# Hybrid Mamba/MoE layer on one core: squares kept in PSUM, other PSUM banks and weight slots around the gate stage, and six products moved from GpSimd to VectorE

## The chip, the cores and the metric

One NeuronCore of a Trainium2 chip. The metric is the device time of one launch in microseconds (us). The names of the engines: PE is TensorE, ACT is ScalarE, DVE is VectorE, POOL is GpSimd, SP issues DMAs.

## The reference, cut to what matters

The layer is `x + mixer(norm(x))`, then a mixture of experts, a block-sparse projection and the same mixture again. The change touches the mixer alone. Per group of heads (8 groups of 16 heads of 64 channels) it computes, cut:

```python
zxbcdt = hidden_states @ in_proj_w.T                    # gate, x, B, C, dt
xBC = silu(causal_conv4(xBC) + conv_b)
Gm = einsum('bcihn,bcjhn->bhcij', C, B)
Y_diag = einsum('bhcij,bcjhd->bcihd', Gm * L, xs)       # L = exp(segment_sum(A dt))
Y_off = einsum('bckhn,bchdn,bhck->bckhd', C, states, state_decay)
y = (Y_diag + Y_off + D * x) * silu(gate)
var = mean(y * y over the group's 1024 channels)
y = y * rsqrt(var + EPS) * norm_w
return y @ out_proj_w.T
```

There are 1024 tokens (2 sequences of 512). `Gm * L` is the decay-score product, `y * y` the squares.

## The kernel before, in words

The whole kernel is one program per engine, written out by hand with counted semaphores; nothing schedules it. The mixer is a loop over the 8 groups (`Fori(0, GROUPS)` in each engine's block). Inside, the order of the work is a fixed sequence of steps, k = 0 to 47 (called ticks here); every engine walks through the same k in its own program and takes from each tick what is its own, so an engine may be several ticks behind another. Semaphores named with `now` wait for a count of this group, `before` for one of the group before; an engine executes strictly in its order, so what stands behind a waiting instruction waits too.

- **Big units** on PE (loop over k, L1515 on): one unit is 12 matmuls of 128x512 into one PSUM bank (3 passes of a hi/lo split times 4 parts of the contraction), or 24 in the output stage. k = 0 to 19 are the convolution inputs (`NCONV`; B, C and eight x tiles, two sequences each), k = 20 to 35 the 16 gate tiles (n = k - 20), k = 36 to 43 the output projection (t = k - 36, halves m = 0 and 1). `big_bank(k)` is k % 3, and unit k waits for whoever reads unit k - 3.
- **Small units** on PE behind each big one, for head units u = 0 to 15: state matmuls at k = u + 10 (bank `ST` = 6), transposes at k = u + 8 (banks 3 and 5), the diagonal matmuls L1603 at k = u + 11 (bank `DG` = 4), which need both decay-score products of u, and the off-diagonal ones L1617 (bank `OF` = 7).
- **ACT**: first tap and tanh of the convolution (L880, L888), the decay tiles (L900, L852), the hi parts of weights (L862), tanh of the gate (L912), the squares (L925) at tick n + 22, and the hi parts `ah` of the output stage (L933).
- **DVE**: taps and the end of the convolution (L1184, L1193: unit k is finished in DVE's tick k + 1), `xs` (L1152), states (L1167, L1172), diagonal and off-diagonal results (L1209, L1215), the gate's (tanh + 1) * gate (L1221) at tick n + 20, the sum of the squares (L1230) at tick n + 23, `al` (L1233), and the lo parts of the output weights (L1139), one per tick.
- **POOL**: y += off-diagonal (L652), `xd` (L664), both decay-score products of a unit (L678, at tick u + 10, counted by `lg_ok`), lo parts of weights (L685), y *= gate (L702, at tick n + 21).

A square goes to `acc` for the first two gate tiles, else to `sq`, half of the SBUF tile `quad`, two slots; DVE adds it to `acc` two steps later:

```python
dst = sq[:, n % 2, :] if tile else acc[:, b, :]
```

Weights pass through 11 slots (`W_SLOT`) at ticks given by `W_TICK`; the last of the eight output pieces has tick 36.

Of the kernel before, what the change touches and what calls it, by code (L numbers as in the profile page):

```python
# [33 lines left out]
def hybrid_layer(nc, x_d, wconv_d, wgate_d, wout_d, wdt_d, cpar_d, gpar_d, dtb_d, alog_d,  # L34
# [8 lines left out]
    with ctx:  # L43
# [30 lines left out]
        sq = quad[:, 0, :].rearrange("p (n s) -> p n s", n=2)  # L74
# [67 lines left out]
        TR, DG, ST, OF = (3, 5), 4, 6, 7  # L142

# [74 lines left out]
        lg_ok = counted("lg_ok", 2 * UNITS)  # L218
# [85 lines left out]
        def phase_end(eng, n):  # L304
# [6 lines left out]
        W_SLOT = [0, 1, 2, 3, 4, 5, 6, 7, 8, 9, 2, 3, 4, 5, 0, 1, 8, 9, 2, 3, 4, 5, 6, 7, 10, 8]  # L311
# [4 lines left out]
            + [28, 29, 30, 31, 32, 33, 34, 36]  # L316
# [26 lines left out]

        def big_bank(k):
            return k % 3

        def big_bank_free(eng, i, k):

            q, wait = (k - 3, now) if k >= 3 else (max(q for q in range(NBIG) if q % 3 == k), before)
            if q < NCONV:  # L350
                wait(eng, conv_ok, i, q + 1)
            elif q < NCONV + NGATE:
                wait(eng, gate_ok, i, q - NCONV + 1)
            else:
                wait(eng, res_ok, i, q - NCONV - NGATE + 1)
# [241 lines left out]
        def _(pool):  # L597
# [45 lines left out]
            with pool.Fori(0, GROUPS) as i:  # L643
                for k in range(NBIG + 4):
# [114 lines left out]
        def _(act):  # L759
# [69 lines left out]
            with act.Fori(0, GROUPS) as i:  # L829
                for k in range(NBIG + 4):  # L830

                    if k - T_G in (1, 2):
                        b = k - T_G - 1
                        tr_done(act, i, f"G{b}")
                        if b == 0:
                            before(act, lg_ok, i, 2 * UNITS)
                        inc(nc.scalar.activation(G[:, b * CH:(b + 1) * CH, :], b4(tr_bank(f"G{b}")), ACT.Copy,
                                                 scale=0.25), g_act)
# [15 lines left out]
                    for p in range(PIECES):  # L854
                        if W_TICK[p] == k:
                            raw_arrived(act, i, p)
                            w_slot_free(act, i, p)
                            kt = p - (PIECES - XT)
                            if kt == 0:
                                act.wait_ge(gpar_in, 16 * (i + 1))  # L860
                            scale = gpar[:, kt:kt + 1] if kt >= 0 else 1.0
                            inc(nc.scalar.activation(wh[:, W_SLOT[p], :], raw[:, R_SLOT[p], :], ACT.Copy,  # L862
                                                     scale=scale), w_hi)

                    if k < NCONV:
# [156 lines left out]
        def _(dve):  # L1022
            credit(dve, (wo_lo, ss_add, taps, conv_ok, xs_ok, s_step, s_ok, off_ok, ydiag_ok, gate_ok, dcol_ok,
# [108 lines left out]
            with dve.Fori(0, GROUPS) as i:  # L1132
                for k in range(NBIG + 4):

                    for p in range(PIECES - XT, PIECES):
                        if W_TICK[p] == k:
                            kt = p - (PIECES - XT)
                            now(dve, w_hi, i, p + 1)
                            inc(STT(wl[:, W_SLOT[p], :], raw[:, R_SLOT[p], :], gpar[:, kt:kt + 1],  # L1139
                                    wh[:, W_SLOT[p], :], ALU.mult, ALU.subtract), wo_lo)  # L1140

# [75 lines left out]

                    if NCONV <= k < NCONV + NGATE:
# [5 lines left out]
                    n = k - 3 - NCONV  # L1224
                    if BATCH <= n < NGATE:
                        b = GATES[n][1]
                        now(dve, sq_ok, i, n + 1)
                        if n > BATCH:
                            now(dve, ss_add, i, n - BATCH)
                        inc(TTn(acc[:, b, :], acc[:, b, :], sq[:, n % 2, :], ALU.add), ss_add)  # L1230
# [230 lines left out]
        def _(pe):  # L1461
# [49 lines left out]
            with pe.Fori(0, GROUPS) as i:  # L1511
                for k in range(NBIG):
# [38 lines left out]
                    if 0 <= u < UNITS:  # L1551
# [4 lines left out]
                        else:  # L1556
                            before(pe, s_ok, i, UNITS)
# [300 lines left out]
```

How the kernel before makes its waits and increments, by code:

```python
        def row_arrived(eng, i, n):  # L246
            q = n % LR
            eng.wait_ge(row_in[q], (i * len(range(q, 2 * UNITS, LR)) + n // LR + 1) * 16)
# [1 line left out]
        def e_arrived(eng, i, u):  # L250
            q = u % ER
            eng.wait_ge(e_in[q], (i * len(range(q, UNITS, ER)) + u // ER + 1) * 32)
# [39 lines left out]
        def now(eng, name, i, n):  # L292
            eng.wait_ge(per[name][0], per[name][1] * (i + 1) + n)
# [1 line left out]
        def before(eng, name, i, n):  # L296
            eng.wait_ge(per[name][0], per[name][1] * i + n)
# [5 lines left out]
        def phase_end(eng, n):  # L304
            eng.drain().then_inc(phase, 1)
            eng.wait_ge(phase, 4 * n)
# [26 lines left out]
        def raw_arrived(eng, i, p):  # L334
            n = R_SLOT[p]
            eng.wait_ge(raw_in[n], (i * R_COUNT[n] + R_SLOT[:p + 1].count(n)) * 16)
# [105 lines left out]
        @block.sync  # L442
        def _(sp):
            xv = x_d.rearrange("(t p) h -> p t h", p=P)
            for n in range(4):
                sp.dma_start(X[:, 2 * n:2 * n + 2, :], xv[:, 2 * n:2 * n + 2, :]).then_inc(x_in[n], 16)
            sp.dma_start(raw[:, 3, :], wdt_d).then_inc(dtw_in, 16)
            sp.dma_start(dtb[:, :], dtb_d).then_inc(par_in, 16)
            sp.dma_start(alog[:, :], alog_d).then_inc(par_in, 16)
            sp.dma_start(rraw[:, :, :], wr_d).then_inc(rt_in, 16)
            sp.wait_ge(dve_self, 1)
            with sp.Fori(0, GROUPS) as i:
                before(sp, taps, i, 3 * NCONV)
# [515 lines left out]
            def t_rows_evac(run, tau):  # L970
                act.wait_ge(tx_mm, job(run, tau) + 1)
                if tau >= 2:
```

## Time and profile before

| | us |
|---|---|
| median of 3 runs (2179.29 to 2180.45) | 2179.96 |
| the profiled execution | 2181.42 |
| its span, first to last instruction | 2179.7 |
| PE busy / DVE / ACT / POOL | 2003.3 / 1502.7 / 1178.5 / 1086.9 |
| one group of the mixer | 207 to 209, eight of them |

The mixer's eight groups take about 1.67 ms of the 2.18. PE is busy 92% of the span, and its granted clock is 0.976 of full speed on average. Starts are in microseconds from the first instruction. Matmuls overlap, so each is shown longer (0.39) than the distance to the next (0.227). "Idle before, releaser" names the instruction whose end let the waiting one go.

### The profile page before, as it was taken

Reading aid. Unit: us, or ns where it says so; the run is one execution under the profiler, and the core shown is the slowest. Engines: PE = TensorE matmul, PEld = TensorE weight load, DVE = VectorE, ACT = ScalarE, POOL = GpSimd, SP = SyncE. Lnnn points to the kernel's source line nnn. Section 1 sums busy time; section 2 is a strip of 40 time slices with the busy share of each in tenths; the row PEclk is TensorE's granted clock in tenths of the full one; section 3 lists DMA queues with packets and bytes.
Section 4 is the critical chain, followed back from the end, with each engine's and each line's share of the span. In section 5 each row is a group of like instructions: output and inputs, shape, how many; then the busy total and the mean of one; then the engine's idle time right before and its main releaser. Section 6 shows DMA issues by size and latency. Waiting matters only on the chain.

```text
span 2179.7 us, 39183 instructions
## 1 busy us (share of the span) xinstructions
PE 2003.3 (92%) x11776; PEld 1645.3 (75%) x11776; DVE 1502.7 (69%) x2710; ACT 1178.5 (54%) x2553; POOL 1086.9 (50%) x955
## 2 busy tenths in 40 slices
PE   3899999999999999999999999999998889978997
PEld 2687778778877887788778877877787667765775
DVE  6698589849884977597669757984988551286214
ACT  2596368537843874396449636953784225321441
POOL 1288149705951693179228814971596025330423
PEclk7899999999999999999999999999999999999999
DMA  2452035114411341233134203511351149923894
GB/s 83 127 154 85 20 117 162 48 42 121 155 49 60 110 138 40 85 119 103 40 89 151 82 26 107 164 57 33 125 160 29 59 163 383 326 60 111 295 386 141
DMA packets 143908, 261.75 MB, mean 120 GB/s; under 512 B 19536, under 2 KB 35920, under 8 KB 143696
## 3 DMA queue, kind: packets, MB, share of 16 engines
q1 hardware_dynamic: 134848, 231.35, 32.8%
q0 software_dynamic: 7520, 24.65, 3.5%
q10 hardware_dynamic: 1328, 3.15, 0.4%
q8 instruction: 106, 1.74, 0.3%
q14 instruction: 106, 0.87, 0.1%
HBM read 233.38 MB, written 25.69 MB: 119 GB/s over the span
## 4 chain that ended last, share of the span: by engine, by line
PE 31%; DVE 31%; issue 23%; POOL 11%; ACT 2%; DVEq 1%; DMA 1%; another core or an unknown queue 1%; POOLq 0%; ACTq 0%; SPq 0%
PE bank L1470 20%; DVE Y L1184 7%; PE bank L1753 5%; POOL Y L702 4%; DVE Y L1193 3%; PE bank L1765 3%; DVE mem L1172 2%; DVE cv L1230 2%; DVE E L1215 2%; DVE mem L1152 2%; DVE Y L1209 2%; POOL wl L685 2%; POOL mem L678 1%; POOL mem L664 1%; DVE gt L1221 1%
## 5 line engine op out<-in xcount | busy, mean ns | idle before, releaser
L1470 PE MATMUL bank<-xh,wh 128*128 128x512 f32 x1288 | 525.9, 408 | 31.4 <-DVE quad L1193 13.3
L1470 PE MATMUL bank<-xh,wl 128*128 128x512 f32 x1288 | 505.3, 392 | 0.0
L1470 PE MATMUL bank<-xl,wh 128*128 128x512 f32 x1288 | 503.3, 391 | 0.0
L685 POOL TENSOR_TENSOR wl<-raw,wh 128x512 fp32r<-128x512 f32 x144 | 184.5, 1286 | 518.9 <-ACT wh L862 518.9
L1470 PEld LDWEIGHTS bank<-xh,wh 128*128 128x128 f32 x1288 | 243.3, 189 | 88.2 <-DVE quad L1193 20.4
L1184 DVE SCALAR_TENSOR_TENSOR Y<-bank,cpar,Y 128x511 f32<-128x511 f32 (+2 forms) x384 | 287.0, 747 | 31.6 <-ACT Y L880 22.6
L1470 PE MATMUL bank<-wh,ah 128*128 128x512 f32 x576 | 235.6, 409 | 54.2 <-DVE al L1233 27.5
L1470 PEld LDWEIGHTS bank<-xh,wl 128*128 128x128 f32 x1288 | 242.6, 188 | 54.2
L1470 PEld LDWEIGHTS bank<-xl,wh 128*128 128x128 f32 x1288 | 243.8, 189 | 45.3 <-issue 0.5
L702 POOL TENSOR_TENSOR Y<-Y,gt 128x512 f32<-128x512 f32 x128 | 197.1, 1542 | 83.7 <-DVE gt L1221 83.7
L1233 DVE TENSOR_TENSOR al<-Y,ah 128x512 fp32r<-128x512 f32 x128 | 105.3, 828 | 188.9 <-ACT ah L933 188.9
L1470 PE MATMUL bank<-wl,ah 128*128 128x512 f32 x576 | 229.9, 399 | 0.0
L1470 PE MATMUL bank<-wh,al 128*128 128x512 f32 x576 | 229.5, 398 | 0.0
L933 ACT ACTIVATE ah<-Y 128x512 fp32r<-128x512 f32 x128 | 79.5, 627 | 220.7 <-PE bank L1470 220.7
L1470 PEld LDWEIGHTS bank<-wh,ah 128*128 128x128 f32 x576 | 111.7, 194 | 90.8 <-issue 37.4
L678 POOL TENSOR_TENSOR mem<-mem,quad 128x512 f32<-128x512 f32 x128 | 163.2, 1299 | 0.0
L717 POOL DMA_INDIRECT cv<-xn_dram,toks x62 | 63.4, 1022 | 193.2 <-DVE toks L1377 107.7
L652 POOL TENSOR_TENSOR Y<-Y,E 128x384 f32<-128x384 f32 x128 | 129.8, 1014 | 54.4 <-DVE E L1215 54.4
L900 ACT ACTIVATE mem<-mem,hpt 128x128 f32<-128x128 f32 x512 | 156.2, 392 | 0.0
L880 ACT ACTIVATE Y<-bank,cpar 128x512 f32<-128x512 f32 x128 | 99.2, 775 | 104.1 <-PE bank L1470 103.9
L912 ACT ACTIVATE gt<-bank 128x512 f32<-128x512 f32 x128 | 76.2, 595 | 117.6 <-POOL Y L702 105.6
L664 POOL TENSOR_TENSOR mem<-mem,hpt 128x384 f32<-128x384 f32 x128 | 107.5, 840 | 63.2 <-DVE mem L1152 63.2
(214 smaller groups left out, 3963.1 us busy)
## 6 DMA issues: line engine op xcount, KB each, us to landing
mem<-c_rows SPq DMA_DIRECT2D x128, 256.0 KB, 3.7
mem<-wffn_d SPq DMA_DIRECT2D x62, 512.0 KB
E<-e_rows SPq DMA_DIRECT2D x256, 96.0 KB, 3.4
raw<-wconv_d SPq DMA_DIRECT2D x80, 256.0 KB, 2.7
cv<-c_rows SPq DMA_DIRECT2D x64, 256.0 KB, 4.1
spare<-c_rows SPq DMA_DIRECT2D x64, 256.0 KB, 4.0
raw<-wgate_d SPq DMA_DIRECT2D x64, 256.0 KB, 2.7
raw<-wout_d SPq DMA_DIRECT2D x64, 256.0 KB, 2.6
```

The source lines that it names most:

```text
L652: inc(pool.tensor_tensor(dst, dst, E[:, u % ER, :], ALU.add), y_ok)
L664: inc(pool.tensor_tensor(xd[:, u % 2, :, :].rearrange("p c (h d) -> p c h d", d=HD), xs[:, u % 3, 0:CH - 1, :].rearrange("p c (h d) -> p c ...
L678: inc(pool.tensor_tensor(L[n % LR], L[n % LR], G[:, b * CH:(b + 1) * CH, :].rearrange("p c i -> p (c i)"), ALU.mult), lg_ok)
L685: inc(pool.tensor_tensor(wl[:, W_SLOT[p], :], raw[:, R_SLOT[p], :], wh[:, W_SLOT[p], :], ALU.subtract), w_lo)
L702: inc(pool.tensor_tensor(dst, dst, gt[:, n % 2, :], ALU.mult), y_gated)
L880: inc(nc.scalar.activation(dst, bank[big_bank(k)][:, :], ACT.Identity, scale=cpar[:, tile, TAPS - 1:TAPS], bias=cpar[:, tile, TAPS:TAPS + ...
L900: last = nc.scalar.activation(L[n % LR][:, c * P:(c + 1) * P], L[n % LR][:, c * P:(c + 1) * P], ACT.Relu, scale=-1.0, bias=hp[:, b * CH + ...
L933: inc(nc.scalar.activation(ah[:, m, :, :], rows_of(t, m), ACT.Copy), y_hi)
L1184: last = STT(dst[:, s:SEQ], bank[big_bank(k)][:, 0:SEQ - s], cpar[:, tile, TAPS - 1 - s:TAPS - s], dst[:, s:SEQ], ALU.mult, ALU.add)
L1233: inc(TTn(al[:, m, :, :], rows_of(t, m), ah[:, m, :, :], ALU.subtract), y_lo)
L1470: got = mm(out, l, r, start=first and n == 0, stop=last and n == 2)
L1753: last = mm(bank[2 + tau % 2][:, a * P:(a + 1) * P], tgu[tau % GU_RING][:, a, kt * P:(kt + 1) * P], xT[tau % 2][:, kt, :], start=kt == 0, ...
```

## The change

Five edits, all in the mixer:

1. The squares of n >= 2 go to PSUM: to bank 0 for n < 8, then to banks 4 and 7 in turn (`DG`, `OF`, whose head units are over by then). Each waits until its bank is free: with one bank, square n waits for the addition of square n - 1.
2. DVE adds a square before the gate instruction of the same tick, not behind it.
3. Big units use a table of banks. k = 0, 1, 2 take banks 6, 7, 4; k = 3 to 19 take (k - 2) % 3; the gate tiles n = 0 to 7 alternate between banks 1 and 2; from n = 8 they rotate over 1, 2, 0 again.
4. The output weights' slots are reordered, and the last piece moves from tick 36 to 35, behind the gate instruction on ACT and DVE.
5. For u = 10 to 15 POOL makes only the first decay-score product; the second is DVE's, behind L1215 of tick u + 10, counted by a new semaphore `lg1_ok`.

```diff
-        sq = quad[:, 0, :].rearrange("p (n s) -> p n s", n=2)
+        def sq(n):
+            return bank[SQ_BANK if n < SQ_LATE else (DG, OF)[n % 2]][:, :]
...
+        LATE = 10
-        lg_ok = counted("lg_ok", 2 * UNITS)
+        lg_ok = counted("lg_ok", UNITS + LATE)
+        lg1_ok = counted("lg1_ok", UNITS - LATE)
...
-        W_SLOT = [0, 1, 2, 3, 4, 5, 6, 7, 8, 9, 2, 3, 4, 5, 0, 1, 8, 9, 2, 3, 4, 5, 6, 7, 10, 8]
+        W_SLOT = [0, 1, 2, 3, 4, 5, 6, 7, 8, 9, 2, 3, 4, 5, 0, 1, 8, 9, 6, 7, 10, 2, 3, 4, 5, 8]
-            + [28, 29, 30, 31, 32, 33, 34, 36]
+            + [28, 29, 30, 31, 32, 33, 34, 35]
...
+        SQ_BANK, SQ_LATE = 0, 8
+        BANKS = [ST, OF, DG] + [(k - 2) % 3 for k in range(3, NCONV)] \
+            + [1 + n % 2 if n < SQ_LATE else (n - SQ_LATE + 1) % 3 for n in range(NGATE)] + [t % 3 for t in range(TT)]
         def big_bank(k):
-            return k % 3
+            return BANKS[k]
         def big_bank_free(eng, i, k):
-            q, wait = (k - 3, now) if k >= 3 else (max(q for q in range(NBIG) if q % 3 == k), before)
+            if k < 3:
+                before(eng, (s_ok, off_ok, ydiag_ok)[k], i, UNITS)
+                before(eng, ss_add, i, NGATE - BATCH)
+                return
+            if k == NCONV + SQ_LATE + 2:
+                now(eng, ss_add, i, SQ_LATE - BATCH)
+                return
+            same = [q for q in range(NBIG) if BANKS[q] == BANKS[k]]
+            q, wait = (max(q for q in same if q < k), now) if min(same) < k else (max(same), before)
...
# POOL, products of the decay and the scores
-                        for h in range(2):
+                        for h in range(2 if u < LATE else 1):
...
# ACT, squares
-                        if n >= 2 * BATCH:
-                            now(act, ss_add, i, n - 2 * BATCH + 1)
-                        dst = sq[:, n % 2, :] if tile else acc[:, b, :]
+                        if n == BATCH:
+                            now(act, conv_ok, i, NCONV - 2)
+                        elif BATCH < n < SQ_LATE:
+                            now(act, ss_add, i, n - BATCH)
+                        elif n >= SQ_LATE + 2:
+                            now(act, ss_add, i, n - 2 - BATCH + 1)
+                        elif n == SQ_LATE:
+                            now(act, ydiag_ok, i, UNITS)
+                        elif n == SQ_LATE + 1:
+                            now(act, off_ok, i, UNITS)
+                        dst = sq(n) if n >= BATCH else acc[:, b, :]
...
# DVE
+                    u = k - A_ - 1
+                    if LATE <= u < UNITS:
+                        pair, b = unit(u)
+                        n = 2 * u + 1
+                        now(dve, decay_ok, i, n + 1)
+                        if u == LATE:
+                            now(dve, g_ok, i, 2)
+                        inc(TTn(L[n % LR], L[n % LR], G[:, b * CH:(b + 1) * CH, :].rearrange("p c i -> p (c i)"),
+                                ALU.mult), lg1_ok)
+                    n = k - 3 - NCONV
+                    if BATCH <= n < NGATE:
+                        b = GATES[n][1]
+                        now(dve, sq_ok, i, n + 1)
+                        if n > BATCH:
+                            now(dve, ss_add, i, n - BATCH)
+                        inc(TTn(acc[:, b, :], acc[:, b, :], sq(n), ALU.add), ss_add)
                     if NCONV <= k < NCONV + NGATE:
                         n = k - NCONV
                         now(dve, gate_th, i, n + 1)
                         last = STT(gt[:, n % 2, :], gt[:, n % 2, :], 1.0, bank[big_bank(k)][:, :],
                                    ALU.add, ALU.mult)
                         inc(last, gate_ok)
-                    n = k - 3 - NCONV
-                    if BATCH <= n < NGATE:
...
-                        inc(TTn(acc[:, b, :], acc[:, b, :], sq[:, n % 2, :], ALU.add), ss_add)
```

Three places of the order of instructions. First DVE in ticks 25 and 26 of a group, before:

```order
L1215 SCALAR_TENSOR_TENSOR E<-bank7,E 128x384 [waits e_in2,off_mm]
L1221 SCALAR_TENSOR_TENSOR gt<-gt,bank1 128x512 [waits gate_th]
L1230 TENSOR_TENSOR cv<-cv,quad 128x512 [waits sq_ok]
L1209 SCALAR_TENSOR_TENSOR Y<-Y,dcol,bank4 128x512 [waits diag_mm]
L252 ISA [waits off_mm]
L1215 SCALAR_TENSOR_TENSOR E<-bank7,E 128x384 [waits e_in0]
L1221 SCALAR_TENSOR_TENSOR gt<-gt,bank2 128x512 [waits gate_th]
```

The same place with the change (lines are those of the changed kernel; `spare,quad` is decay tile times scores, `cv` the sum of squares):

```order
L1248 SCALAR_TENSOR_TENSOR E<-bank7,E 128x384 [waits e_in2,off_mm]
L1258 TENSOR_TENSOR spare<-spare,quad 128x512 [waits decay_ok]
L1267 TENSOR_TENSOR cv<-cv,bank0 128x512 [waits sq_ok]
L1271 SCALAR_TENSOR_TENSOR gt<-gt,bank2 128x512 [waits gate_th]
L1242 SCALAR_TENSOR_TENSOR Y<-Y,dcol,bank4 128x512 [waits diag_mm]
L256 ISA [waits off_mm]
L1248 SCALAR_TENSOR_TENSOR E<-bank7,E 128x384 [waits e_in0]
```

The product (L1258) is new between the off-diagonal result and the gate instruction, in ticks 20 to 25; the addition of the square reads a bank and stands ahead of the gate instruction. The second place is DVE in ticks 29 and 30 with the change:

```order
L1271 SCALAR_TENSOR_TENSOR gt<-gt,bank2 128x512 [waits gate_th]
L298 REGISTER_ALU
L1166 SCALAR_TENSOR_TENSOR wl<-raw,gpar,wh 128x512 [waits w_hi]
L298 REGISTER_ALU [waits sq_ok]
L1267 TENSOR_TENSOR cv<-cv,bank0 128x512 [waits ss_add]
L1271 SCALAR_TENSOR_TENSOR gt<-gt,bank0 128x512 [waits gate_th]
```

The first row is the gate instruction of n = 9, the last that of n = 10; the addition between them is that of square 7, the last square in bank 0. The third place is PE from the end of unit 29 to the start of unit 30 (n = 10) with the change:

```order
L1516 MATMUL bank<-xh,wh 128x512
L1516 MATMUL bank<-xl,wh 128x512
L1516 MATMUL bank<-xh,wl 128x512
L298 ISA
L1516 MATMUL bank<-xh,wh 128x512 [waits ss_add]
```

Before, unit 30 waited for `gate_ok` of unit 27; now it waits for the addition of square 7.

## Rows read from the trace of the kernel before

**Rows 1.** Waits of PE in the whole span: releaser, us in total, times, longest.

```profile
PE bank L1470 <- DVE quad L1193: 13.3, 16, 1.1
PE bank L1603 <- POOL cv L678: 10.6, 8, 1.3
PE bank L1603 <- POOL mem L678: 8.4, 8, 1.1
PE bank L1470 <- DVE al L1233: 27.5, 24, 1.6
PE bank L1470 <- DVE wl L1139: 4.0, 8, 0.5
```

**Rows 2.** The chain in order of time, one big unit of PE: start, us.

```profile
899.99 2.73 PE bank L1470 x12
```

**Rows 3.** Timeline, PE, start of the output stage, fifth group: start, us, [idle before].

```profile
1053.61 0.49 PE L1470 MATMUL bank<-wh,ah 128*128 128x512 f32 x1 [1.37 <-DVE al L1233]
...
1062.49 0.47 PE L1470 MATMUL bank<-wh,ah 128*128 128x512 f32 x1 [1.64 <-DVE al L1233]
```

**Rows 4.** Window, output stage: us, busy of PE, PEld, DVE, ACT, POOL, PEclk.

```profile
core 0 of [0], span 2179.7 us
...
1064.00:1066.00 2.00, 2.00 (x7) 1.52 (x5) 0.00 (x0) 0.00 (x0) 0.00 (x0) 0.50 0.52 149
```

**Rows 5.** Timeline, POOL, tick 23 of the fifth group.

```profile
1010.01 1.04 POOL L652 TENSOR_TENSOR Y<-Y,E 128x384 f32<-128x384 f32 x1
1010.98 0.86 POOL L664 TENSOR_TENSOR mem<-mem,hpt 128x384 f32<-128x384 f32 x1
1011.77 2.53 POOL L678 TENSOR_TENSOR mem<-mem,quad 128x512 f32<-128x512 f32 x2
1014.24 1.30 POOL L685 TENSOR_TENSOR wl<-raw,wh 128x512 fp32r<-128x512 f32 x1
1015.46 1.32 POOL L702 TENSOR_TENSOR Y<-Y,gt 128x512 f32<-128x512 f32 x1
```

**Rows 6.** Timeline, PE, state matmuls of two ticks one behind the other.

```profile
1006.74 0.83 PE L1560 MATMUL bank<-mem,quad 128*128 128x128 f32 x6
...
1012.50 0.83 PE L1560 MATMUL bank<-mem,quad 128*128 128x128 f32 x6
```

**Rows 7.** Timeline, PE's end of tick 19 and DVE's end of convolution unit 18.

```profile
985.92 0.94 PE L1617 MATMUL bank<-quad,mem 128*128 128x128 f32 x6
...
989.12 0.68 DVE L1193 SCALAR_TENSOR_TENSOR Y<-bank,Y 128x512 f32<-128x512 f32 x1
```

**Rows 8.** Timeline, ACT and DVE in the gate ticks of the fifth group.

```profile
1036.03 0.60 ACT L912 ACTIVATE gt<-bank 128x512 f32<-128x512 f32 x1 [0.50 <-PE bank L1470]
...
1037.19 0.63 ACT L925 ACTIVATE quad<-Y 128x512 f32<-128x512 f32 x1 [0.56 <-DVE cv L1230]
...
1037.73 0.71 ACT L862 ACTIVATE wh<-raw,gpar 128x512 fp32r<-128x512 f32 x1
...
1035.88 0.67 DVE L1221 SCALAR_TENSOR_TENSOR gt<-gt,bank 128x512 f32<-128x512 f32 x1
...
1053.29 0.74 DVE L1139 SCALAR_TENSOR_TENSOR wl<-raw,gpar,wh 128x512 fp32r<-128x512 f32 x1
```

**Rows 9.** Timeline, DVE's first addition of a square, and POOL meanwhile.

```profile
1024.13 5.57 DVE L1230 TENSOR_TENSOR cv<-cv,quad 128x512 f32<-128x512 f32 x1
...
1023.12 2.58 POOL L678 TENSOR_TENSOR spare<-spare,quad 128x512 f32<-128x512 f32 x2
...
1027.81 1.34 POOL L702 TENSOR_TENSOR Y<-Y,gt 128x512 f32<-128x512 f32 x1
```

**Rows 10.** Timeline, a later addition; and VectorE between queued POOL instructions, second mixture.

```profile
1033.06 1.19 DVE L1230 TENSOR_TENSOR cv<-cv,quad 128x512 f32<-128x512 f32 x1
...
1944.52 1.51 DVE L1067 TENSOR_SCALAR cv<-X,mv,rs 128x512 f32<-128x512 f32 x1
...
1944.27 2.90 POOL L710 TENSOR_TENSOR wl<-raw,wh 128x512 fp32r<-128x512 f32 x2
```

More of the change, by code:

```diff
@@ L829, in _, with weight_hi @@
             with act.Fori(0, GROUPS) as i:
+                def weight_hi(p):
+                    raw_arrived(act, i, p)
+                    w_slot_free(act, i, p)
+                    kt = p - (PIECES - XT)
+                    if kt == 0:
+                        act.wait_ge(gpar_in, 16 * (i + 1))
+                    scale = gpar[:, kt:kt + 1] if kt >= 0 else 1.0
+                    inc(nc.scalar.activation(wh[:, W_SLOT[p], :], raw[:, R_SLOT[p], :], ACT.Copy,
+                                             scale=scale), w_hi)
                 for k in range(NBIG + 4):
@@ L835, in _ @@
                         if b == 0:
-                            before(act, lg_ok, i, 2 * UNITS)
+                            before(act, lg_ok, i, UNITS + LATE)
+                            before(act, lg1_ok, i, UNITS - LATE)
                         inc(nc.scalar.activation(G[:, b * CH:(b + 1) * CH, :], b4(tr_bank(f"G{b}")), ACT.Copy,
@@ L852, in _ @@
                             inc(nc.scalar.activation(L[n % LR], L[n % LR], ACT.Exp, scale=-1.0), decay_ok)
-                    for p in range(PIECES):
+                    for p in range(PIECES - 1):
                         if W_TICK[p] == k:
[L856 to L863, printed above, removed]
+                            weight_hi(p)
                     if k < NCONV:
@@ L875, in _ @@
                             before(act, tr_mm, i, 4)
-                            before(act, ss_add, i, NGATE - BATCH)
                         elif tile == 1:
@@ L913, in _ @@
                                                  scale=0.5), gate_th)
+                    if k == W_TICK[PIECES - 1]:
+                        weight_hi(PIECES - 1)
                     ks = k - 2
@@ L1022, in _ @@
         def _(dve):
-            credit(dve, (wo_lo, ss_add, taps, conv_ok, xs_ok, s_step, s_ok, off_ok, ydiag_ok, gate_ok, dcol_ok,
+            credit(dve, (wo_lo, lg1_ok, ss_add, taps, conv_ok, xs_ok, s_step, s_ok, off_ok, ydiag_ok, gate_ok, dcol_ok,
                          nrm_ok, y_lo, res_ok, f_hg, f_h, a_lo, dn_acc))
@@ L1132, in _, with out_weight_lo @@
             with dve.Fori(0, GROUPS) as i:
+                def out_weight_lo(p):
+                    kt = p - (PIECES - XT)
+                    now(dve, w_hi, i, p + 1)
+                    inc(STT(wl[:, W_SLOT[p], :], raw[:, R_SLOT[p], :], gpar[:, kt:kt + 1],
+                            wh[:, W_SLOT[p], :], ALU.mult, ALU.subtract), wo_lo)
                 for k in range(NBIG + 4):
-                    for p in range(PIECES - XT, PIECES):
+                    for p in range(PIECES - XT, PIECES - 1):
                         if W_TICK[p] == k:
[L1137 to L1140, printed above, removed]
+                            out_weight_lo(p)
                     u = k - (B_ - 1)
@@ L1223, in _ @@
                         inc(last, gate_ok)
-                    n = k - 3 - NCONV
-                    if BATCH <= n < NGATE:
[L1226 to L1229, printed above, removed]
-                        inc(TTn(acc[:, b, :], acc[:, b, :], sq[:, n % 2, :], ALU.add), ss_add)
+                    if k == W_TICK[PIECES - 1]:
+                        out_weight_lo(PIECES - 1)
                     for t, m in y_evac(k):
@@ L1556, in _ @@
                         else:
-                            before(pe, s_ok, i, UNITS)
+                            now(pe, conv_ok, i, 3)
                             now(pe, tr_act, i, 2)
@@ L1594, in _ @@
                         pair, b = unit(u)
-                        now(pe, lg_ok, i, 2 * u + 2)
+                        now(pe, lg_ok, i, 2 * u + 2 if u < LATE else u + LATE + 1)
+                        if u >= LATE:
+                            now(pe, lg1_ok, i, u - LATE + 1)
                         if u:
```

## The prediction

> **What bounds the kernel now.** I read the page first: PE is busy 92% of the span, so what can be gained is the time in which PE stands. The list of PE's waits [rows 1] says where that is in the mixer. There are four places, each in all eight groups, and each has its end on DVE or POOL. (a) At a group's start PE waits twice for the end of a convolution unit (DVE L1193), 13.3 us in all. (b) The diagonal matmuls wait for POOL's decay-score products (L678), 10.6 + 8.4 = 19.0 us. (c) The output stage's first pieces wait for `al` (L1233), 27.5 us, and (d) for the last output weight (L1139), 4.0 us. Then I read the timeline around them. A big unit takes PE 2.73 us [rows 2]; a full tick with the small units takes 5.76 (1012.50 - 1006.74, [rows 6]). In ticks 21 to 23 POOL needs 0.97 + 0.79 + 2.47 + 1.22 + 1.24 = 6.7 us a tick [rows 5], more than PE; that is wait (b). In the output stage the second unit starts 8.88 us after the first (1062.49 - 1053.61, [rows 3]) where two halves of PE's work need 5.46, and the first started 1.37 late: 4.8 us lost in a group.
>
> The two reasons behind (c) are the port that DVE and POOL share and DVE's order. The first addition of a square lasted 5.57 us where 0.68 is normal [rows 9], the same in all eight groups; others waited half a microsecond [rows 10]. This holds the squares, and with them ACT's `ah`, back.
>
> **The change, part by part.** All in us for a group; eight groups.
>
> *Early banks.* Units 3 to 5 go to banks that nobody reads, so the two waits of (a) go: 13.3 in all, and with the restarts about 15 (lower end 13, upper 18 if the 0.2 us wait of a later unit goes too). DVE is idle for about 4 us among these ticks, so it can follow; POOL and ACT idle there. **-15.** What is late next: unit 6 still waits for convolution unit 3.
>
> *Two banks for gate tiles 0 to 7.* Unit 20 goes to bank 1, whose last user is unit 18, no longer unit 17. DVE ends unit 18 at 989.12 + 0.68 = 989.80; PE's tick 19 starts its last six matmuls at 985.92 and would go on at 986.6 [rows 7]. PE now waits 3.2 there. DVE and PE both need 5.76 a tick in this stretch, so neither edit before it closes that lag. Bounds: 2.0 if DVE has run ahead by then, 3.2. I take 3.2: **+26.** The later tiles wait for the gate instruction two units back, which comes 0.1 + 0.60 + 0.67 after a unit's end [rows 8], under 2.73: nothing.
>
> *Products.* POOL's ticks 20 to 25 lose one product of 1.24 and come to 5.5, under 5.76, and the wait at unit 20 gives POOL three more microseconds. The 19.0 of (b) goes, **-19**, if DVE gets its product done in time. DVE's tick there is 0.6 + 1.2 + 0.7 + 0.5 + 0.6, start to start (xs, states, two results, gate), so of PE's 5.76 about 2 us are left. Its product reads two SBUF tiles, as the addition did, and POOL is busy throughout. How long it waits is not shown for this place. The near end is the rest of one POOL instruction, up to 1.24: then DVE's tick is 5.4 and nothing waits. The far end is rows 9, where DVE stood through four starts of POOL and got in when POOL ran dry. I take the near end, because DVE got in at POOL's next hand-over in the two additions that follow (1.19, [rows 10]) in every group, and in the second mixture three times running, although POOL's next instruction had its input long before (1.51 us at 1944.52, while POOL went from one L710 to the next, [rows 10]). The far end is the first rival.
>
> The Trainium skill, page "SBUF — State Buffer", section "SBUF: two separate sides", says that the pair shared by VectorE and GpSimd is an exclusive lock that whichever starts first has for its whole instruction. By it the wait is one POOL instruction, and the sum is the one below; the trace agrees in rows 10, and disagrees in rows 9, where four instructions passed.
>
> *Squares in PSUM.* The addition then reads one SBUF tile and takes 0.68 with no wait, as the gate instruction does. ACT's square costs the same. But the squares 2 to 7 sit in bank 0, and unit 30 is the next matmul user of it. It waits for the addition of square 7, which DVE makes in its tick 30, behind the gate instruction of unit 29. So PE must finish unit 29 and then wait for a round: ACT starts 0.11 after the end (E), tanh 0.60; gate instruction to E + 1.4; meanwhile ACT's square and the hi weight (0.63, 0.71) are done at E + 1.9, POOL's multiply has the port from E + 1.5 to E + 2.7; lo weight 0.74, addition 0.68, PE goes on at E + 4.0 [rows 8]. PE would have gone on at E - 0.16, so it stands 4.1. Bounds: 3.4 if the lo weight does not meet POOL, 4.6 if DVE comes half a microsecond late. **+33.** Nothing hides it, for no other work of PE lies there.
>
> *Output stage.* In the gate ticks DVE took 2.9 a tick (from one gate instruction, as the one at 1035.88 in [rows 8], to the next) because addition, POOL's multiply and lo weight take turns at the port; PE needs 2.73, and DVE fell behind. Now the addition is out of that turn, the wait at unit 30 lets DVE and ACT catch up, and the last lo weight comes at E + 2.1 of unit 35 where PE wants it at E + 4.8. The first `al` come before unit 35 ends. The third waits for square 15, which needs POOL's last multiply: E + 5.3 by my chain, with PE ready at the same time; I leave 0.3. So 4.8 - 0.3 = 4.5: **-36** (ends -38 and -12). The slots change no wait: the pieces of ticks 28 to 30 get slots that are free earlier, and those of 31 to 34 get slots free since tick 28.
>
> *Clock.* After these waits the granted clock was 0.50 for some 3 us, the lower level of 1.2 GHz [rows 4], in five of the eight groups, about 1.7 each. The new pause at unit 30 is as long as the old ones together, so I leave it: 0, ends -9 and +5.
>
> Sum: -15 + 26 - 19 + 33 - 36 = **-11**. Against the profiled execution (2181.42, span 2179.7, [rows 4]) that is 2170.4; it lies 1.5 above the median of the runs, so I predict **2169.0**. With the ends of the terms, this case alone lies at 2153 to 2183.
>
> **The rivals.** A measurement of this kernel can tell 0.2%, 4.4 us, from no change.
>
> 1. *POOL keeps the port (slower).* If DVE's product waits until POOL has nothing queued, as in rows 9, then DVE and POOL take turns: POOL runs 0.97 + 0.79 + 1.24 + 1.22 + 1.24 = 5.5 until it needs `xs`, which stands behind the product in DVE's order; then product, gate instruction and `xs`, 1.95 with the hand-overs. The tick is 7.4, against PE's 5.76. It decides as soon as the product waits for more than two POOL instructions (2.5 us), for DVE has 2 to spare. The first such product (u = 11) is 2.1 late, three ticks add 4.9, 1.6 of that was lost before too: +5.4 a group in place of +3.2 - 2.4. That is 4.6 x 8 = 37 more: **2206**. For it: all eight first additions, and the same instruction kind. Against it: rows 10. Chance 0.28.
> 2. *The waits at units 20 and 30 are smaller.* DVE gains on PE at the group's start and keeps it; half of 26 and a third of 33 go: **2145**. Against it: DVE has no idle time in ticks 11 to 19. Chance 0.10.
> 3. *The output stage's wait only moves.* DVE's lo weights and `al` still wait for POOL's multiply, and the chain of square 15 remains. Then 1.5 of 4.8 is gained, 24 less: **2193**; half of that loss gives 2181, no change. Chance 0.12.
>
> **How the numbers follow.** The forecast has 0.50. It is above 2175.6 or so in one case in seven of its own (0.06 within 0.2%, 0.01 slower). Faster: 0.43 + 0.10 = 0.53. Within 0.2%: 0.06 + 0.04 = 0.10. Slower: 0.28 + 0.08 + 0.01 = 0.37. The range goes to the first rival with a little beyond and most of the way to the second: 2150 to 2208, leaving out about 0.07 on each side.
>
> **What would show it.** Right: the convolution waits at units 3 and 5 gone; a PE wait of about 3.2 at unit 20, released by the end of a convolution unit on DVE; one of about 4 at unit 30, released by the addition; additions all 0.68; new products of 0.7 to 1.9; diagonal matmuls with no wait; output stage's first two units 5.5 apart. Wrong: products of 3 to 5 us and waits of 1 to 5 us before the diagonal matmuls (rival 1), or a wait at unit 30 under 2 us, or output units still over 7 apart.

## The result, and the profile after

The changed kernel takes **2193.3 us** (median of four runs, 2185.8 to 2196.2); the kernel before takes 2180.2 (2179.3 to 2180.9). The ratio is 1.0052 (95% interval 1.0029 to 1.0075): **0.5% slower**. In a later comparison, beside other kernels, it was 1.0054 (1.0041 to 1.0067). I had said 2169, faster; the right sign was in the range, but not in the forecast.

The four runs already say something that their median doesn't. Their mean granted clocks are 0.967, 0.966, 0.962 and 0.963, and the two with the higher clock are the two fastest. The kernel before had 0.976. The profile is of the fastest run (2185.8, span 2184.0), so it shows the difference at its smallest.

The list of PE's waits of the changed kernel (releaser, us in total, times, longest):

```profile
core 0 of [0], span 2184.0 us
...
PE bank L1516 <- DVE cv L1267: 38.1, 8, 4.8
PE bank L1516 <- DVE Y L1226: 25.7, 16, 3.1
PE bank L1516 <- DVE al L1443: 17.9, 4, 9.1
...
PE bank L1516 <- POOL wl L701: 14.2, 8, 8.0
...
PE bank L1516 <- DVE quad L1226: 3.8, 8, 0.5
```

Against [rows 1]: the waits for convolution units at a group's start (13.3) have become one of 0.48 at unit 6 (3.8). The waits for POOL's products (10.6 + 8.4), for `al` (27.5) and for the last output weight (4.0) are gone. New are 3.04 a group at unit 20, for the end of a convolution unit (L1226; 0.17 of each pair is the old wait of a later unit), and 4.76 a group at unit 30, for DVE's addition of square 7 (L1267). These are the waits that I had announced, at the places that I had announced. The waits of the mixer come to 81.8 where they were 78.3 before (both with the group starts, 10.5 + 2.5 before and 14.2 now, and with the 1.5 of later convolution units before); the list's other waits fell by 10.

How long the mixer itself takes stands in two rows of PE: its first matmul, and the first one of the norm behind it, which in both kernels comes after the same 6.84 of waiting. Before:

```profile
64.20 0.79 PE L1470 MATMUL bank<-xh,wh 128*128 128x512 f32 x1 [7.92 <-POOL wl L685]
...
1732.12 2.79 PE L1478 MATMUL bank<-ident,Y 128*128 128x128 f32 x12 [6.84 <-DVE Y L1067]
```

With the change:

```profile
61.81 0.79 PE L1516 MATMUL bank<-xh,wh 128*128 128x512 f32 x1 [8.01 <-POOL wl L701]
...
1741.42 2.79 PE L1524 MATMUL bank<-ident,Y 128*128 128x128 f32 x12 [6.84 <-DVE Y L1097]
```

That is 1667.9 and 1679.6, so +11.7 for the mixer (+9.1 in a second profile of the change). The rest of the launch, which the change does not touch, is 7.4 shorter in this profile (511.8 and 504.4); so the two spans are only 4.3 apart.

The tile views of DVE's new products and of its additions (ns: min/median/max):

```profile
L1258 DVE TENSOR_TENSOR mem<-mem,quad x16: 835/886/944, 175.3 to 1642.3; 128x512 f32<-128x512 f32 x16
L1258 DVE TENSOR_TENSOR cv<-cv,quad x16: 681/1107/1559, 163.9 to 1647.6; 128x512 f32<-128x512 f32 x16
L1258 DVE TENSOR_TENSOR spare<-spare,quad x16: 682/1014/1366, 169.6 to 1652.8; 128x512 f32<-128x512 f32 x16
L1267 DVE TENSOR_TENSOR cv<-cv,bank x112: 672/675/690, 192.3 to 1695.6; 128x512 f32<-128x512 f32 x112
```

All 48 products take 0.68 to 1.56 us, so none waited for more than one instruction of POOL. All additions take 0.68; the 5.57 of [rows 9] has no counterpart.

What I had not seen is behind unit 30. The timeline of PE in the fifth group (start, us, idle before):

```profile
1042.20 0.79 PE L1516 MATMUL bank<-xh,wh 128*128 128x512 f32 x1 [4.76 <-DVE cv L1267]
1042.79 0.63 PE L1516 MATMUL bank<-xl,wh 128*128 128x512 f32 x1
1043.22 0.63 PE L1516 MATMUL bank<-xh,wl 128*128 128x512 f32 x1
...
1046.97 0.39 PE L1516 MATMUL bank<-xh,wl 128*128 128x512 f32 x1
1047.20 0.39 PE L1516 MATMUL bank<-xh,wh 128*128 128x512 f32 x1
```

The twelve matmuls of the unit take from 1042.20 to 1047.20, 5.00 us, where [rows 2] has 2.73. The windows of the same stretch (us; PE, PEld, DVE, ACT, POOL busy; granted clock; DMA):

```profile
1035.00:1040.00 5.00, 2.44 (x11) 1.69 (x9) 3.93 (x6) 3.19 (x6) 1.55 (x2) 1.00 0.32 70
1040.00:1045.00 5.00, 2.80 (x7) 2.22 (x8) 1.78 (x2) 0.33 (x1) 0.99 (x1) 0.50 0.30 88
1045.00:1050.00 5.00, 5.00 (x20) 4.04 (x19) 1.45 (x2) 1.73 (x3) 1.13 (x1) 0.81 0.01 2
1050.00:1055.00 5.00, 5.00 (x24) 4.14 (x23) 4.93 (x7) 3.45 (x6) 1.46 (x2) 1.00 0.27 61
```

The granted clock is 0.50, the 1.2 GHz level, when PE restarts, and is full again 4.7 us later (0.81 from 1045 on is 1.9 us at 0.50; the matmuls take 0.39 again from 1046.97 on). In windows of this kind over the whole mixer it falls behind unit 30 in all eight groups, and behind unit 20 in three. Before, it fell in five of eight groups, behind the waits of the output stage. So the theory to test had two parts: the waits of the mixer came out near even, and the loss is the half clock that the two pauses bring. The rival: PE's pauses only stand for a lag of DVE, ACT and POOL, which would come back elsewhere if they were taken away.

### The profile page after: what moved, and what is told of

It is laid out like the page before. It is cut to its first block, busy times and chain, and to the rows that moved or that the text cites. A ratio compares the mean times of both kernels' runs of the same rounds, so it can differ in the third digit from the quotient of the medians.

```text
span 2184.0 us, 39232 instructions
## 1 busy us (share of the span) xinstructions
PE 2012.7 (92%) x11776; PEld 1661.3 (76%) x11776; DVE 1463.7 (67%) x2758; ACT 1176.8 (54%) x2553; POOL 1026.9 (47%) x907
## 4 chain that ended last, share of the span: by engine, by line
PE 37%; issue 28%; DVE 27%; POOL 5%; ACT 1%; DMA 1%; DVEq 1%; POOLq 0%; SPq 0%; ACTq 0%
PE bank L1516 20%; DVE Y L1217 7%; PE bank L1801 5%; POOL Y L718 4%; DVE Y L1226 3%; PE bank L1651 3%; PE bank L1813 3%; DVE mem L1205 2%; PE bank L1665 2%; DVE mem L1185 2%; DVE E L1248 2%; DVE quad L1217 2%; PE bank L1606 1%; DVE Y L1242 1%; PE bank L1788 1%
## 5 line engine op out<-in xcount | busy, mean ns | idle before, releaser
L1516 PE MATMUL bank<-xh,wh 128*128 128x512 f32 x1288 | 534.0, 415 | 85.4 <-DVE cv L1267 38.1
L1516 PE MATMUL bank<-xh,wl 128*128 128x512 f32 x1288 | 512.7, 398 | 0.0
L1516 PE MATMUL bank<-xl,wh 128*128 128x512 f32 x1288 | 511.6, 397 | 0.0
L1516 PEld LDWEIGHTS bank<-xh,wh 128*128 128x128 f32 x1288 | 248.5, 193 | 144.3 <-DVE cv L1267 41.4
L1516 PEld LDWEIGHTS bank<-xl,wh 128*128 128x128 f32 x1288 | 248.8, 193 | 47.1 <-issue 0.5
L718 POOL TENSOR_TENSOR Y<-Y,gt 128x512 f32<-128x512 f32 x128 | 182.5, 1426 | 156.6 <-DVE gt L1271 154.8
L1516 PE MATMUL bank<-wh,ah 128*128 128x512 f32 x576 | 230.3, 400 | 18.6 <-DVE al L1443 17.9
L1279 DVE TENSOR_TENSOR al<-Y,ah 128x512 fp32r<-128x512 f32 x128 | 95.6, 747 | 188.3 <-ACT ah L963 188.3
L668 POOL TENSOR_TENSOR Y<-Y,E 128x384 f32<-128x384 f32 x128 | 141.3, 1104 | 75.0 <-DVE E L1248 75.0
L694 POOL TENSOR_TENSOR mem<-mem,quad 128x512 f32<-128x512 f32 x112 | 142.5, 1292 | 0.0
```

The lines of the kernel that those rows point to most:

```text
L668: inc(pool.tensor_tensor(dst, dst, E[:, u % ER, :], ALU.add), y_ok)
L694: inc(pool.tensor_tensor(L[n % LR], L[n % LR], G[:, b * CH:(b + 1) * CH, :].rearrange("p c i -> p (c i)"), ALU.mult), lg_ok)
L718: inc(pool.tensor_tensor(dst, dst, gt[:, n % 2, :], ALU.mult), y_gated)
L1279: inc(TTn(al[:, m, :, :], rows_of(t, m), ah[:, m, :, :], ALU.subtract), y_lo)
L1516: got = mm(out, l, r, start=first and n == 0, stop=last and n == 2)
```

## Experiments

Twelve runs. All ratios are against the kernel before on the same chip, whose medians were 2175.1 to 2184.8; with them stands the 95% interval. "Low clock" counts the groups in which a window of 5 us behind the named unit was granted under 0.97. The first few us of the mixer, behind PE's wait of about 8 us for its first weights, are at 0.50 in every kernel and are not counted.

### 1. Taking the two waits away

The gate tiles n = 8 to 15 go on alternating between banks 1 and 2, and the wait for the addition moves to unit 36, the first output unit:

```
+ BANKS = [...] + [1 + n % 2 for n in range(NGATE)] + [t % 3 for t in range(TT)]
- if k == NCONV + SQ_LATE + 2:
+ if k == NCONV + NGATE:
      now(eng, ss_add, i, SQ_LATE - BATCH)
```

> The change, but all sixteen gate tiles alternate between banks 1 and 2, so that no gate unit takes bank 0 after the squares; the first output unit (unit 36) is the first to take it. Theory 1 (pause and clock both cost): the 4.76 us wait at unit 30 goes in all eight groups (-38), the output stage gets no new wait of more than 1 us, and the stretch at half clock that followed unit 30 in eight of eight groups goes too (another -10 to -20): 2135 to 2150 against 2193 for the change. Theory 2 (the pause only let DVE, ACT and POOL catch up): their lag comes back at the output stage, as the wait for al (27.5 us before): about 2180, and the half clock moves there.

Measured: 2141.4, ratio 0.9809 (0.9789 to 0.9828), that is 53 us less than the changed kernel by the ratios (1.0052 - 0.9809 = 0.0243 of 2180). The wait is gone and nothing took its place in the output stage: its list of waits has no `al` L1279. 38 of the 53 were the wait itself. Behind unit 30 no group has low clock any more; behind unit 20, whose wait is still there, five have it, where the change has three. This is what theory 1 says: the pause and the clock both cost time, and no lag comes back elsewhere.

The other edit leaves unit 30 alone and gives unit 20 bank 0 (last user unit 17):

```
+ [(0, 1, 2)[n] if n < 3 else 2 - n % 2 if n < SQ_LATE + 2 else (0, 2, 1)[(n - SQ_LATE - 2) % 3] ...]
- if n == BATCH: now(act, conv_ok, i, NCONV - 2)
+ if n == BATCH: now(act, gate_ok, i, 1)
```

> The change, but the first gate tile (unit 20) goes to bank 0, whose last user is unit 17, and the first square in PSUM waits for that tile's gate instruction; unit 30 still waits for the addition of square 7. Theory 1: the 3.04 us wait at unit 20 goes in eight groups (-24) and nothing takes its place: 2165 to 2172 against 2193. Theory 2 (DVE and PE are both full in the ticks behind unit 20, so a lag of DVE that is not waited for at unit 20 is waited for at the diagonal matmuls or is added to the wait at unit 30): less than half of the 24 is gained, 2181 to 2190, with new waits for the products or a wait at unit 30 over 6 us.

Measured: 2158.0, 0.9878 (0.9860 to 0.9897): 38 less than the changed kernel, more than I expected: 24.3 are the wait, about 4 the low clock that followed unit 20 in three groups, and the rest is not explained. The wait at unit 30 stayed as it was:

```profile
PE bank L1516 <- DVE cv L1267: 38.1, 8, 4.8
```

and the low clock behind it came in eight of eight groups. So DVE's lag is not passed on from unit 20 to unit 30; the second theory has no support here either.

Both edits together:

```
+ BANKS = [...] + [0] + [2 - n % 2 for n in range(1, NGATE)] + [t % 3 for t in range(TT)]
```

> The change with both bank edits: unit 20 on bank 0, every other gate tile alternating between banks 2 and 1. Theory 1: both waits and the half clock behind unit 30 go: 2105 to 2130, under both kernels, PE's waits in the mixer under 15 us in all. Theory 2: gains of the two single edits do not add, because without any pause DVE falls behind: 2150 to 2175, with one wait of 2 to 5 us a group at the output stage.

Measured: **2105.6, 0.9638 (0.9622 to 0.9655)**, 90 under the changed kernel and 79 under the one before; it beats both kernels. The gains of the two single edits (53 + 38 = 91) add up. Its waits:

```profile
core 0 of [0], span 2107.7 us
...
PE bank L1516 <- POOL wl L701: 13.9, 8, 8.0
...
PE bank L1516 <- DVE quad L1226: 3.8, 8, 0.5
...
PE bank L1516 <- DVE Y L1226: 1.3, 8, 0.2
```

The rest of the mixer has none; its mean clock is 0.978. No window of the mixer is low behind its start; the next low one lies where PE waits 6.84 us for the norm.

### 2. The clock by itself

Which part of that is clock? This kernel keeps every wait of the change and only gives PE something to do in the pause:

```
+ if k == NCONV + SQ_LATE + 2:
+     now(pe, xs_ok, i, UNITS)
+     for f in range(18):
+         mm(bank[TR[1]][:, :], xh[:, f % KT, 0:P], xh[:, f % KT, b * SEQ:(b + 1) * SEQ], start=True, stop=True)
  big_bank_free(pe, i, k)
```

> The change, with 18 more matmuls of 128x512 per group, whose result nobody reads: TensorE makes them into an idle transpose bank ahead of its wait at unit 30 (about 4.1 of the 4.76 us at 0.23 each). Every wait of the change stays where it is. If the idle time is what brings the half clock behind unit 30 (theory 1), the eight stretches of low clock there go and the time falls by 8 to 16, to 2177 to 2185, with TensorE still resuming unit 30 when the addition ends. If the low clock comes from elsewhere (rival), the time stays within 4 of the change.

Beside it, on another chip, the change once more:

> The change once more, beside the kernel before on another chip, to set the filled kernel and the parts against it. The clock behind unit 30 should be low in at least seven of the eight groups again; ratio 1.000 to 1.007.

Measured: filled 0.9996 (0.9987 to 1.0005), the change 1.0054 (1.0041 to 1.0067). **More work on PE, and 0.58% less time: 12.6 us.** The restart at unit 30 of the filled kernel, and its windows at the same place:

```profile
1034.48 4.24 PE L1580 MATMUL bank<-xh 128*128 128x512 f32 x18
1039.43 0.51 PE L1517 MATMUL bank<-xh,wh 128*128 128x512 f32 x1 [0.71 <-DVE cv L1268]
```

```profile
1035.00:1040.00 5.00, 4.29 (x19) 3.24 (x18) 3.66 (x5) 1.61 (x3) 1.41 (x2) 1.00 0.16 52
1040.00:1045.00 5.00, 5.00 (x23) 4.12 (x22) 1.32 (x2) 1.73 (x3) 1.00 (x1) 1.00 0.16 57
```

4.24 of unread matmuls and 0.71 of waiting: the addition comes no earlier, but the first matmul takes 0.51 in place of 0.79, and the clock stays full in eight of eight groups. What is left is low clock behind unit 20, in five groups (three and one in the two profiles of the change), so a part of the gain at unit 30 is lost again there. The second fill goes there:

```
+ if k == NCONV:
+     now(pe, conv_ok, i, 18)
+     for f in range(12):
+         mm(bank[0][:, :], xh[:, f % KT, 0:P], xh[:, f % KT, b * SEQ:(b + 1) * SEQ], start=True, stop=True)
```

> The kernel with the filled pause at unit 30, and in each group 12 more unread matmuls of 128x512 (2.7 us) into bank 0 ahead of the wait at unit 20 (3.04 us). In the kernel filled at unit 30 alone, low clock still followed unit 20 in four or five of eight groups. If idle TensorE is the cause there too, those stretches go and a further 4 to 8 us are gained (ratio 0.996 to 0.998 against 0.9996); the mean granted clock comes to 0.978 or more, that of the kernel with both bank edits, and what is left above that kernel is the waits alone (62 us). If nothing changes, the low clock behind unit 20 has another cause.

Measured: 0.9948 (0.9930 to 0.9967), 2171.5 where before had 2183.9; mean clock of its runs 0.977 to 0.982. The waits at unit 20 are filled (they were 25.7 with those of the later unit):

```profile
PE bank L1517 <- DVE Y L1227: 3.6, 16, 0.3
```

No window of the mixer is low. That is another 0.48%, 10 us, more than expected; the two intervals are 0.2% apart, so the size is uncertain, the sign isn't. Together the two fills give back 23 us. The kernel then lies 68 above the one with both bank edits (0.9948 - 0.9638), and the two waits, which it keeps in full length, are 38.1 + 24.3 = 62 of that.

The last piece of this is a wait of half the length. Unit 31 in place of unit 30 takes bank 0:

```
+ BANKS = [...] + [1 + n % 2 if n < SQ_LATE + 3 else (0, 1, 2)[(n - SQ_LATE - 3) % 3] ...] + [(t + 2) % 3 ...]
- if k == NCONV + SQ_LATE + 2:
+ if k == NCONV + SQ_LATE + 3:
```

> The change, but unit 31 instead of unit 30 is the first to take bank 0 behind the squares. DVE's addition of square 7 stays where it is, so TensorE spends one more big unit (2.73 us) before it waits. Theory 1: the wait shrinks from 4.76 to about 2.0 in each group (-22), and with the half clock less often or shorter (-5 to -15): 2155 to 2166. If it is the addition that moves along with TensorE's unit (rival: DVE's order decides and the lag is carried on), the wait stays over 4 us and the time within 5 of the change.

Measured: 2160.8, 0.9932 (0.9919 to 0.9946), 26 less than the change.

```profile
core 0 of [0], span 2159.0 us
...
PE bank L1516 <- DVE cv L1267: 16.4, 8, 2.1
...
PE bank L1516 <- DVE al L1279: 4.3, 8, 0.6
```

The wait is 2.05 in place of 4.76 (-21.7), with 0.54 a group of the output stage's wait back (+4.3). Low clock follows unit 31 in two groups of eight, where it followed unit 30 in eight. (It followed unit 20 in all eight here.) Of the 26 the waits are 17.

### 3. The parts of the change alone

Early banks alone, in the kernel before:

```
- return k % 3
+ return ([ST, OF, DG] + [(k - 2) % 3 for k in range(3, NBIG)])[k]
```

> The kernel before with one part alone: units 0 to 2 take the banks of states, off-diagonal and diagonal results, units 3 to 5 find their banks free; everything else as before, gate units on three banks. The waits of 1.10 and 0.56 us at units 3 and 5 go, one of 0.48 at unit 6 comes: -9 to -10, about 2170 against 2180 (ratio 0.9955). My forecast of -15 would be 0.993. If PE's earlier arrival only brings it to later waits on POOL's products, the gain is under 4.

Measured: 2156.4, 0.9912 (0.9897 to 0.9927): 19 us. The wait at unit 6 (3.8) is there, so 9.5 us of the gain are waits of the mixer (13.3 - 3.8). The waits of the output stage are as before:

```profile
core 0 of [0], span 2154.8 us
PE bank L1476 <- DVE al L1239: 27.6, 24, 1.6
...
PE bank L1476 <- DVE quad L1199: 3.8, 8, 0.5
```

and yet no window behind them is low, where five were before; the mean clock is 0.979 against 0.976. In the kernel before, twelve matmuls behind the last wait of the output stage take 4.2 to 4.4 in these five groups and 2.8 in the other three, 7.7 in all; with the 9.5 this makes 17 of the 19. So my -15 was too low in time and too high in waits (13.3 of it), and why the same 1.6 us waits no longer bring the low clock isn't settled here.

Squares in PSUM alone, with slots and order of the change and all products on POOL:

```
+ SQ_BANK = 2
+ BANKS = [k % 3 for k in range(NCONV)] + [2] + [(n + 1) % 2 for n in range(1, NGATE)] + [(t + 2) % 3 for t in range(TT)]
```

> The kernel before with one part alone: squares in PSUM on bank 2, gate tiles alternating between banks 0 and 1 behind a first one on bank 2, the slots and the addition's place of the change; products all on POOL, early banks not. By differences between the earlier runs (79 for all three parts, 10 for the early banks, 21 to 24 for the products) it should be 45 to 50 under the kernel before, ratio 0.977 to 0.980. By the waits of the output stage alone it would be 31 under it, ratio 0.986, which would leave some 15 us for an interaction of the parts.

Measured: 2132.3, 0.9794 (0.9781 to 0.9808): 45 us. 31.5 of them are the output stage's waits, which are gone, and no window of the mixer is low, where the five of before cost 7.7; the runs' clocks are 0.978 to 0.983.

The products alone, squares in SBUF and banks as before; the first two lines are POOL's, the third is DVE's, for u = 10 to 15:

```
- for h in range(2):                 
+ for h in range(2 if u < 10 else 1):
+ inc(TTn(L[n % LR], L[n % LR], G[...], ALU.mult), lg1_ok)
```

> The kernel before with one part alone: from the eleventh head unit on VectorE makes the second of the two products; squares stay in SBUF, banks as before. If VectorE always gets the shared port at POOL's next hand-over in this place (forecast), all 48 products last under 1.9 us, the waits on POOL's products go and the time falls by 15 to 25 (ratio 0.988 to 0.993). If the first addition's long wait (5.57 us, rows 9) comes from POOL's queue of ready work at that tick, it should get shorter than 4 us here, since POOL then has one product less in tick 26; if it stays above 5 us, the length of POOL's queue is not its cause. First rival of the prediction: products of 3 us and more, slower than before.

Measured: 2138.0, 0.9827 (0.9814 to 0.9840): **38 us, twice the waits on POOL's products.** Two rows say why, the waits and DVE's additions (ns: min/median/max):

```profile
PE bank L1483 <- DVE al L1246: 15.8, 16, 1.6
```

```profile
L1243 DVE TENSOR_TENSOR cv<-cv,quad x112: 677/680/1198, 190.8 to 1644.4; 128x512 f32<-128x512 f32 x112
```

The wait for `al` fell from 27.5 to 15.8 with the squares still in SBUF, and the longest addition is 1.20 and not 5.57. That the shorter addition brings the shorter wait is the likely reason; no run separates the two. Low clock follows the output stage in three groups here, where it was five. Its products last up to 1.86:

```profile
L1228 DVE TENSOR_TENSOR spare<-spare,quad x16: 1707/1747/1856, 166.8 to 1606.8; 128x512 f32<-128x512 f32 x16
```

The two edits that I had given a term each do part of the same work. The sums show it, all parts with the two good banks:

| kernel | ratio | us of 2180 |
|---|---|---|
| early banks | 0.9912 | -19 |
| products | 0.9827 | -38 |
| squares | 0.9794 | -45 |
| squares + early banks | 0.9736 | -58 |
| squares + products | 0.9710 | -63 |
| all three | 0.9638 | -79 |
| all three, banks as changed | 1.0052 | +11 |

The two pairs are the kernel with both bank edits, less one part. Without the products:

```
- LATE = 10
+ LATE = UNITS
```

> As the kernel with both bank edits, but POOL makes all decay-score products as before. If the products moved to DVE are worth what the waits on POOL's products were (19.0 us before), this comes out 15 to 25 slower than the kernel with both bank edits and shows the waits of 0.4 to 1 us before the diagonal matmuls again. The rival: in the kernel with both edits DVE is the engine that is late, then its products cost as much as they save and the two kernels agree within 5 us.

Measured: 2129.3, 0.9736 (0.9718 to 0.9754); the waits for POOL's products are back at 10.6 and 8.4. On top of the others the products are worth 21 us.

Without the early banks:

```
- BANKS = [ST, OF, DG] + [(k - 2) % 3 for k in range(3, NCONV)] + ...
+ BANKS = [k % 3 for k in range(NCONV)] + ...
```

> The kernel with both bank edits, but units 0 to 5 on three banks as before (products on VectorE, squares in PSUM). Early banks alone gave 19 us; if the parts add, this is 2124 to 2130 where the kernel with all parts has 2106 (ratio 0.972 to 0.975). If the early banks' gain beyond the 13.3 us of waits was clock that the other waits had spoiled, it is less here: 9 to 14, ratio 0.968 to 0.970.

The squares go to bank 2 here, as in the kernel with the squares alone. Measured: 2113.2, 0.9710 (0.9697 to 0.9722). On top of the others the early banks are worth 16, between the two guesses. Squares and products together give 63 where their sum is 83: 20 us are counted twice.

## Why the prediction was wrong

Its forecast was 2169 and the measurement 2193: -11 announced, +11 measured by the ratio, +11.7 for the mixer in the profile. Term by term, with the waits of the profile of the change for eight groups:

- *Clock, 0 with ends -9 and +5: this is the step that failed.* I wrote that "the new pause at unit 30 is as long as the old ones together, so I leave it". The old ones are four waits (1.37, 0.46, 0.50, 1.64) with matmuls between them; the new ones are 4.76 and 3.04 in one piece. Twelve matmuls behind unit 30 take 4.2 to 5.3 in the eight groups, against 2.89 in the filled kernel: 17.2 more. Behind unit 20 the three slow groups add 4.3. The slow stretches of before, which are gone, were 7.7. So the term that I put at 0 is +14 in the profile. Filled, the two pauses give 12.6 and about 10 us back. With both filled the ratio is 0.9948, which is -11 on 2180: the sum that I had for the kernel without a clock term. That match is partly luck, as the next points show, but without the slow restarts the same change with the same waits is faster than the kernel before; with them it is slower.
- *Squares in PSUM, the wait at unit 30, +33: measured 38.1 (4.76 each, outside my 3.4 to 4.6).* The mechanism was right; my chain left a link out. Squares 2 to 7 share one bank, so each square also waits for the addition of the one before. DVE and ACT in the fifth group of the change:

```profile
1037.26 1.19 DVE L1166 SCALAR_TENSOR_TENSOR wl<-raw,gpar,wh 128x512 fp32r<-128x512 f32 x1 [0.71 <-ACT wh L853]
1038.38 0.68 DVE L1267 TENSOR_TENSOR cv<-cv,bank 128x512 f32<-128x512 f32 x1
...
1040.36 1.18 DVE L1166 SCALAR_TENSOR_TENSOR wl<-raw,gpar,wh 128x512 fp32r<-128x512 f32 x1 [0.71 <-ACT wh L853]
1041.47 0.68 DVE L1267 TENSOR_TENSOR cv<-cv,bank 128x512 f32<-128x512 f32 x1
```

```profile
1039.09 0.60 ACT L955 ACTIVATE bank<-Y 128x512 f32<-128x512 f32 x1 [0.94 <-DVE cv L1267]
1039.62 0.71 ACT L853 ACTIVATE wh<-raw,gpar 128x512 fp32r<-128x512 f32 x1
```

```profile
1039.73 1.27 POOL L718 TENSOR_TENSOR Y<-Y,gt 128x512 f32<-128x512 f32 x1 [1.82 <-DVE gt L1271]
```

  Lo weight, addition, square, hi weight, lo weight is a ring of 1040.36 - 1037.26 = 3.10 us, longer than PE's 2.73. I had the hi weight done 1.9 behind the end of unit 29 (1037.44), it is done at 2.9; and the lo weight met POOL's multiply, which ends at 1041.00 (1.18, not 0.74). No run gives squares 2 to 7 a second bank; that the ring makes the difference is read from these rows and not tested.
- *Two banks for gate tiles 0 to 7, +26: measured 24.3,* 3.04 each, at the place and with the releaser that I gave. Right.
- *Products, -19: right in this kernel* (all of these waits are gone, no product above 1.56), *but worth 38 alone.* The first rival, that POOL keeps the port, is refuted: its products of 3 to 5 us occur in no run (the longest is 1.87, in the kernel with unit 20 on bank 0). Its price happened to be near the result, but for another reason.
- *Output stage, -36: right.* None of its waits is left; in the list they were 31.5. My term was counted from unit to unit, with the slower restart behind each wait, and so is the row to set against it:

```profile
1060.82 0.39 PE L1516 MATMUL bank<-wh,ah 128*128 128x512 f32 x1
...
1066.51 0.47 PE L1516 MATMUL bank<-wh,ah 128*128 128x512 f32 x1
```

  The second unit starts 5.69 behind the first, not 8.88, and the first without its 1.37: 4.56 a group, 36.5 in all. My third rival, that this wait only moves, didn't come; that its price, 2193, is the time measured is chance. But the products alone would have brought 11.7 of it, which I had put down to the squares.
- *Early banks, -15: in waits -9.5,* as the 0.48 at unit 6 came, which I had named as what is late next and given no price (13.3 of the 15 were waits, the rest restarts). At a group's start the waits for weights and the last results went from 10.5 + 2.5 to 14.2.
- The second rival, smaller waits at units 20 and 30, is refuted: both have nearly the same length in all eight groups.

Adding up the waits: -9.5 + 24.3 - 19.0 + 38.1 - 31.5 + 1.2 = +3.6 in the mixer. My terms without their restarts (13.3 for 15, 31.5 for 36) were -13.3 + 26 - 19 + 33 - 31.5 = -4.8, so 8 of the miss are waits that I sized too small, at units 30 and 6 above all. The clock is the larger part, +14 in place of 0. The list has 40 waits of PE in the mixer in place of 80; behind a wait at full clock twelve matmuls take about 2.85 and not 2.73, so by estimate -5 for fewer restarts. 3.6 + 13.8 - 5 = 12.4, against 11.7 in the profile. PE's waits outside the mixer came out 10 lower, at places that differ by 5 to 10 us between kernels that don't change them (the FFN's wait for `al` alone ranges from 17 to 26), so I don't count them for the change.

The range of 2150 to 2208 held the result, but the upper end of 2183 that I gave the forecast's own case doesn't follow from the ends of its terms: the output stage's alone (-12 in place of -36) leads to 2193.

The Trainium skill, page "SBUF — State Buffer", section "SBUF: two separate sides", has the port that VectorE and GpSimd share as a lock for one whole instruction. All 48 products of the change agree with it (at most 1.56, so at most 0.88 beside the 0.68 of the work, and POOL's products take 1.29 on average), and those of the kernel with the products alone are under 1.9. The 5.57 of [rows 9] doesn't agree, and stays unexplained. It disappeared when POOL had one product less a tick, but POOL also goes from instruction to instruction without a pause where DVE's products get in at once. A long queue of POOL is then perhaps needed for it; it is not enough.

## What to carry to other kernels

Price a new wait of TensorE by its length in one piece: what several short waits cost is no measure for one long one, and a long pause is paid for twice, by itself and by the slow restart. A good way to tell the two apart is to fill the pause with matmuls that nobody reads. When two edits act on the same queue (here the port of DVE and POOL, on the way to `al`), try each alone before giving each its own term; and when a buffer is moved into a shared bank, look for the first other user of the bank, and choose the rotation so that this user comes late.

## What I had not expected of the hardware

- Behind a pause of 4.76 us TensorE restarted at half clock in 16 of 16 groups (two profiles of the change) and needed 4.2 to 5.3 us for twelve matmuls, where it needed 2.89 at full clock. With 4.24 us of unread matmuls in the pause: in none of eight.
- Behind pauses of 3.0 us the clock fell in one to eight groups of eight, depending on the kernel (three and one in two profiles of the same change, eight with unit 31 as the first user). Behind the output stage's waits of up to 1.6: in five of eight groups before, in three with the products alone, in none with early banks. What decides between these isn't known from these runs.
- Runs of one kernel differ by as much as this: 2185.8 at a mean clock of 0.967, 2196.2 at 0.962.
- A DVE instruction on two SBUF tiles had the port after less than one POOL instruction in 48 of 48 cases in one place, and in another stood for 5.57 us, in each of eight groups.
